# A four-layer transformer block on one core: the layer norms' normalisation on GpSimd, four places for exponentials, and another form of the negated maxima

## The reference

```
x = x + attn0(norm(x))    # one head of 64, causal, biases on q, k, v and out
x = x + ffn0(norm(x))     # x and W rounded to 8-bit e4m3, product in float, plus bias
x = x + attn1(norm(x))    # 16 heads of 16, rotary positions, causal
x = x + ffn1(norm(x))     # token shift: sigmoid(xr Wr) * (relu(xk Wk)^2 Wv)
```

## Time and profile before

| | before |
|---|---|
| median of three runs | 2562.5 us (2561.86 to 2568.54) |
| profiled execution, its own time | 2564.48 us |
| span of its profile | 2562.6 us |
| TensorE busy | 2287.1 us (89%) |
| VectorE busy | 1992.9 us (78%) |
| ScalarE busy | 1512.8 us (59%) |
| GpSimd busy | 528.7 us (21%) |
| mean granted TensorE clock | 0.961 |

### The profile page before, as it was taken

How to read it: one execution, slowest core, us unless ns; L and a number is a source line. 1 busy time by engine, 2 the same in 40 slices (tenths; PEclk the granted TensorE clock), 3 DMA queues, 4 the chain that set the end, 5 groups by cost and what they waited for, 6 DMA issues and landing times.

```text
span 2562.6 us, 51736 instructions
## 1 busy us (share of the span) xinstructions
PE 2287.1 (89%) x19060; PEld 1051.6 (41%) x19060; DVE 1992.9 (78%) x4326; ACT 1512.8 (59%) x2753; POOL 528.7 (21%) x526
## 2 busy tenths in 40 slices
PE   6788878899999999999989999899999989998896
PEld 4444433343444444353434435344344434332344
DVE  4577688888877887879786787887887689889922
ACT  2235437666656657666655565666665567677762
POOL 4444110212114120220304213031211400000011
PEclk7899879999999999999999999999999999999998
DMA  1222211020312222030211302012021121110110
GB/s 47 80 80 71 68 47 43 27 68 17 81 33 50 66 56 60 22 85 12 66 38 37 95 23 80 25 37 70 17 73 33 39 68 45 30 44 23 27 44 27
DMA packets 184102, 125.37 MB, mean 49 GB/s; under 512 B 83120, under 2 KB 183600, under 8 KB 183856
## 3 DMA queue, kind: packets, MB, share of 16 engines
q1 hardware_dynamic: 183088, 121.16, 17.3%
q10 hardware_dynamic: 768, 0.92, 0.1%
HBM read 62.20 MB, written 59.24 MB: 47 GB/s over the span
## 4 chain that ended last, share of the span: by engine, by line
PE 54%; DVE 29%; ACT 6%; issue 5%; DMA 2%; SPq 1%; DVEq 1%; POOL 1%; POOLq 0%; ACTq 0%
DVE mx L1506 20%; PE psum L1815 11%; PE psum L1760 6%; PE psum L1793 5%; PE psum L1726 4%; ACT probs L1266 4%; PE psum L1599 3%; PE psum L1690 2%; PE psum L1846 2%; PE psum L1661 2%; PE psum L1866 2%; PE psum L1835 2%; PE psum L1747 2%; PE psum L1630 2%; DVE xn L1387 2%
## 5 line engine op out<-in xcount | busy, mean ns | idle before, releaser
L1266 ACT ACTIVATE probs<-psum 128x512 f32<-128x512 f32 x2176 | 1142.1, 607 | 506.1 <-PE psum L1793 297.0
L1506 DVE TENSOR_REDUCE mx<-psum 128x1 f32<-128x512 f32 (+2 forms) x2304 | 1285.6, 621 | 143.5 <-PE psum L1760 110.8
L1815 PE MATMUL psum<-probs,vs 128*17 128x512 f32 (+3 forms) x5120 | 592.7, 544 | 3.2 <-ACT probs L1266 2.2
L1760 PE MATMUL psum<-kst,qst 48*128 48x512 f16 (+3 forms) x2560 | 443.5, 356 | 95.7 <-DVE mx L1506 47.3
L1793 PE MATMUL psum<-qst,kst 50*128 50x512 f16 (+3 forms) x2560 | 434.7, 354 | 68.3 <-DVE mx L1506 28.0
L1760 PEld LDWEIGHTS psum<-kst,qst 48*128 48x128 f16 x2560 | 134.0, 94 | 409.4 <-DVE mx L1506 160.8
L1793 PEld LDWEIGHTS psum<-qst,kst 50*128 50x128 f16 x2560 | 130.0, 93 | 384.9 <-ACT probs L1266 150.9
L1815 PEld LDWEIGHTS psum<-probs,vs 128*17 128x17 f32 x5120 | 92.9, 96 | 163.1 <-issue 130.6
L1051 POOL TENSOR_SCALAR vare<-mv 128x4 f32<-128x4 f32 x64 | 15.9, 249 | 682.8 <-DVE mv L1368 682.8
L1767 PE MATMUL psum<-maskq,identh 64*128 64x128 bf16 (+1 forms) x2048 | 133.5, 207 | 0.0
L1080 POOL TENSOR_TENSOR sums<-probs 128x512 f32<-128x512 f32 x12 | 15.3, 1274 | 520.4 <-ACT probs L1220 520.4
(11 more groups left out here) (171 smaller groups left out, 2762.6 us busy)
## 6 DMA issues: line engine op xcount, KB each, us to landing
qk_dram<-parts SPq DMA_DIRECT2D x168, 128.0 KB
qst<-qk_dram SPq DMA_DIRECT2D x128, 96.0 KB, 2.4
kst<-qk_dram SPq DMA_DIRECT2D x128, 96.0 KB, 2.3
v_dram<-vst SPq DMA_DIRECT2D x64, 136.0 KB, 4.6
vs<-v_dram SPq DMA_DIRECT2D x64, 136.0 KB, 2.1
xs<-x_in SPq DMA_DIRECT2D x16, 512.0 KB, 4.1
x_dram<-xs SPq DMA_DIRECT2D x16, 512.0 KB, 2.9
att_dram<-ast SPq DMA_DIRECT2D x64, 128.0 KB, 2.0
```

Of the source, the lines that this page charges most:

```text
L1266: act.activation(dst, src, ACT.Exp, scale=DK1 ** -0.5 / LIFT ** 2).then_inc(S["exp"], 1)
L1506: ins = dve.tensor_reduce(mx1[:, n % 2, 2 * g + odd, tile % TPC, c:c + 1], bank(src, at, at + cols), AX.X, ALU.max)
L1760: ins = pe.matmul(two[odd][:, at:at + cols], qst[rows, qslot, pair, P * (tile % TPC):P * (tile % TPC + 1)], kst[rows, kslot, pair, 0:cols] ...
L1815: ins = pe.matmul(bank(7, off, CH, rows=VW, row=32 * h), vtile[:, h, :], probs[:, HG * (step_no(b, hg, k) % 2) + h, at:at + CH - off], sta ...
```

## The change

- The job `norm` moves from VectorE to GpSimd: the same four `tensor_scalar` instructions with the same waits. Its planned time goes from 1.3 to 2.1 us. The masks that GpSimd makes in the first chunk now come after the first normalisation, and the scaling of late weights on VectorE comes ahead of the statistics instead of the normalisation.
- `probs` gets places for four steps; exponentials wait for the values of step n - 4.
- In `nmax` the odd and even heads are kept apart from the start: two reductions (one for each), one conversion, and one subtraction in place of two. The planned time goes from 0.54 to 0.8 us.
- The layout of the two float16 parts changes with it, so `rows` needs four DMAs of half the size in place of two; planned at 0.3 in place of 0.2 us.
- `out` on VectorE waits for its own job of the block before.

```diff
@@ -42,6 +42,7 @@
 PARTS = 2
 PROWS = len(STORED[0]) * DK1
 LIFT = 4.0
+PSTEPS = 4
 UNIT1 = 32768.0
 REST = 2 * DK1
 MAXROWS = 2
@@ -389,7 +390,7 @@
         add("DVE", "stats", (ln, *c), key(), 1.75, *after, ("norm", same and (ln, *same)), ("root", same and (ln, *same)))
         add("POOL", "root", (ln, *c), key(), 1.33, ("stats", (ln, *c)), ("norm", same and (ln, *same)))
         old = (2, *same) if ln == 0 and same else (ln - 1, *c) if ln else None
-        add("DVE", "norm", (ln, *c), key(), 1.3, ("root", (ln, *c)),
+        add("POOL", "norm", (ln, *c), key(), 2.1, ("root", (ln, *c)),
             ("turn", old))
 
     def turn(ln, *after):
@@ -516,16 +517,16 @@
                 add("DVE", "max d", (*unit, odd), key, 0.07 * reads + 0.533 * size, ("max", unit),
                     ("nmax", block_before(b, hg, q, 2)), free=(("max", unit), odd))
         end = pos - LEAD + UNIT * (q + 1)
-        add("DVE", "nmax", me, end, 0.54, *[("max d", (*unit, odd)) for unit in units for odd in range(2)], ("turnmax", old))
+        add("DVE", "nmax", me, end, 0.8, *[("max d", (*unit, odd)) for unit in units for odd in range(2)], ("turnmax", old))
         add("PE", "turnmax", me, end - 20, 0.07, ("nmax", me), lat=0.1, claim="P", mode="C")
         add("DVE", "turnmax d", me, end - 20, 0.13, ("turnmax", me), ("rows", block_before(b, hg, q, 2)),
             free=("turnmax", me))
-        add("SP", "rows", me, end - 20, 0.2, ("turnmax d", me), lat=2.6)
+        add("SP", "rows", me, end - 20, 0.3, ("turnmax d", me), lat=2.6)
         for k in range(first_step(q), final_step(q) + 1):
             kbs = STEPS[k][1]
             key = pos + UNIT * kbs[0] / TPC
             diagonal = kbs[0] >= TPC * q
-            two = step_before(b, hg, k, 2)
+            two = step_before(b, hg, k, PSTEPS)
             exps = []
             for j, pieces in enumerate(score_jobs(k)):
                 size = sum(cols for *_, cols in pieces) / CH
@@ -584,7 +585,7 @@
     add("DVE", "stats", (3, *c), key(), 1.75, ("add1", (*c, 0)), ("add1", (*c, 1)), ("norm", p and (3, *p)),
         ("root", p and (3, *p)))
     add("POOL", "root", (3, *c), key(), 1.33, ("stats", (3, *c)), ("norm", p and (3, *p)))
-    add("DVE", "norm", (3, *c), key(), 1.3, ("root", (3, *c)), ("turn", p and (3, *p)), ("turn", lent and (2, *lent)))
+    add("POOL", "norm", (3, *c), key(), 2.1, ("root", (3, *c)), ("turn", p and (3, *p)), ("turn", lent and (2, *lent)))
     add("POOL", "carry", c, key(), 0.2, *[("mix", p and (*p, i)) for i in range(2)],
         *[("prod", p and (*p, i)) for i in range(2)])
     turn(3, ("norm", (3, *c)), ("carry", c))
@@ -752,12 +753,12 @@
         kst = sb("kst", [P, KRING, HG // 2, CH], F16)
         qst = sb("qst", [P, QRING, HG // 2, CH], F16)
         vs = sb("vs", [P, 2, NT, HG * VW], F32)
-        probs = sb("probs", [P, 2 * HG, CH], F32)
+        probs = sb("probs", [P, PSTEPS * HG, CH], F32)
         osb = sb("osb", [P, 2, CH], F32)
         ast = sb("ast", [P, 2, TPC, HG * DK1], F32)
         mx1 = sb("mx1", [P, 2, HG, TPC, NQ], F32)
-        nmax1 = sb("nmax1", [P, HG, TPC], F32)
-        nmaxb = sb("nmaxb", [P, 2, MAXROWS, HG // 2, TPC], F16)
+        nmax1 = sb("nmax1", [P, 2, HG // 2, TPC], F32)
+        nmaxb = sb("nmaxb", [P, MAXROWS, 2, HG // 2, TPC], F16)
         nmaxT1 = sb("nmaxT1", [HG * MAXROWS * TPC, 2, P], F16)
         rec = sb("rec", [P, TPC, HG], F32)
 
@@ -831,7 +832,7 @@
 
         def rows_written(wt, b, hg, q):
             n = block_no(b, hg, q)
-            wt.wait_ge(f"rows {n % QRING}", 32 * (n // QRING + 1))
+            wt.wait_ge(f"rows {n % QRING}", 64 * (n // QRING + 1))
 
         def v_loaded(wt, b, hg, c):
             wt.wait_ge(f"load v {hg % 2} {c}", 16 * ((NHG * b + hg) // 2 + 1))
@@ -957,9 +958,10 @@
                     n = block_no(*item)
                     wt.job("turnmax d", item)
                     for odd in range(2):
-                        row = HALF * odd + PROWS
-                        sp.dma_start(qst[row:row + MAXROWS, n % QRING, :, :],
-                                     nmaxT1[16 * odd:16 * (odd + 1), n % 2, :]).then_inc(S[f"rows {n % QRING}"], 16)
+                        for row in range(MAXROWS):
+                            at = 8 * (2 * row + odd)
+                            sp.dma_start(qst[HALF * odd + PROWS + row:HALF * odd + PROWS + row + 1, n % QRING, :, :],
+                                         nmaxT1[at:at + 8, n % 2, :]).then_inc(S[f"rows {n % QRING}"], 16)
                 elif kind == "put att":
                     b, hg, q = item
                     n = block_no(*item)
@@ -1051,11 +1053,29 @@
                     pool.tensor_scalar(vare[:, at, :], mv[:, at, :, 1], EPS, None, ALU.add).then_inc(S["chain p"], 1)
                     wt.wait_ge("chain p", COUNT["root", item])
                     pool.tensor_tensor(rstd[:, at, :], vare[:, at, :], mhalf[:, :], ALU.pow).then_inc(S["root"], 1)
+                    if item != (0, 0, 0) and pieces < KRING:
+                        pool.memset(kst[:, pieces, :, :], UNIT1).then_inc(done, 1)
+                        pieces += 1
+                elif kind == "norm":
+                    ln, b, q = item
+                    old = shared(b, q) if ln < 3 else before(b, q)
+                    at = moments(ln, b, q)
+                    wt.job("root", item)
+                    if ln == 3:
+                        src, dst = xp[:, q % 2, :, :], xn3
+                        wt.job("turn", old and (3, *old))
+                        if (b, q) == (0, 0):
+                            wt.job("turn", (2, 0, NQ - 1))
+                    else:
+                        src, dst = xs[:, q % 2, :, :], xns[lane(b, q)]
+                        earlier = (ln - 1, b, q) if ln else old and (2, *old)
+                        wt.job("turn", earlier)
+                    for t in range(TPC):
+                        ins = pool.tensor_scalar(dst[:, t, :], src[:, t, :], mv[:, at, t, 0:1], rstd[:, at, t:t + 1],
+                                                ALU.subtract, ALU.mult)
+                    ins.then_inc(S["norm"], 1)
                     if item == (0, 0, 0):
                         masks(n)
-                    elif pieces < KRING:
-                        pool.memset(kst[:, pieces, :, :], UNIT1).then_inc(done, 1)
-                        pieces += 1
                 elif kind == "bias0":
                     b, q = item
                     wt.wait_ge("ready", 1)
@@ -1252,10 +1272,10 @@
                                    tiles(home("V1", item), DK1), ACT.Copy).then_inc(S["v1"], 1)
                 elif kind == "exp":
                     b, hg, k, j, odd = item
-                    wt.job("values", step_before(b, hg, k, 2))
+                    wt.job("values", step_before(b, hg, k, PSTEPS))
                     wt.job("scores", item[:4])
                     pieces = score_jobs(k)[j]
-                    at = HG * (step_no(b, hg, k) % 2)
+                    at = HG * (step_no(b, hg, k) % PSTEPS)
                     src = bank(PLAN.home["scores", item[:4]][odd], 0, sum(cols for *_, cols in pieces))
                     if pieces[0][0] == pieces[-1][0]:
                         dst = probs[:, at + 2 * pieces[0][0] + odd, 0:sum(cols for *_, cols in pieces)]
@@ -1349,6 +1369,8 @@
                     old = shared(b, q) if ln < 3 else before(b, q)
                     at = moments(ln, b, q)
                     wt.job("norm", old and (ln, *old))
+                    if item == (3, 0, 0):
+                        later_weights()
                     if ln == 0:
                         x_loaded(wt, b, q)
                     elif ln == 1:
@@ -1367,26 +1389,6 @@
                     for t in range(TPC):
                         ins = dve.bn_aggr(mv[:, at, t, :], stats[:, at, t, :])
                     ins.then_inc(S["stats"], 1)
-                elif kind == "norm":
-                    ln, b, q = item
-                    if item == (3, 0, 0):
-                        later_weights()
-                    old = shared(b, q) if ln < 3 else before(b, q)
-                    at = moments(ln, b, q)
-                    wt.job("root", item)
-                    if ln == 3:
-                        src, dst = xp[:, q % 2, :, :], xn3
-                        wt.job("turn", old and (3, *old))
-                        if (b, q) == (0, 0):
-                            wt.job("turn", (2, 0, NQ - 1))
-                    else:
-                        src, dst = xs[:, q % 2, :, :], xns[lane(b, q)]
-                        earlier = (ln - 1, b, q) if ln else old and (2, *old)
-                        wt.job("turn", earlier)
-                    for t in range(TPC):
-                        ins = dve.tensor_scalar(dst[:, t, :], src[:, t, :], mv[:, at, t, 0:1], rstd[:, at, t:t + 1],
-                                                ALU.subtract, ALU.mult)
-                    ins.then_inc(S["norm"], 1)
                 elif kind == "wf8":
```

(19 more changed lines are left out.)

## The result

| | before | after |
|---|---|---|
| median | 2565.5 us (4 runs) | 2607.8 us (4 runs, 2602.4 to 2614.2) |
| ratio, 95% interval | | 1.0166 [1.0137, 1.0196] |
| profiled execution, its span | 2564.5, 2562.6 us | 2608.1, 2606.0 us |

What follows compares the result with a forecast made beforehand. The prediction took TensorE to bound the kernel, held up in short pieces by a VectorE often one job late. Its terms, -25 + 0 - 5 + 0 - 6 - 3 + 1 = -38, gave 2525 us, range 2492 to 2570.

Steps and rivals of the forecast that it cites:

- part 2: Normalisation joins GpSimd: 0.45 us per instruction, 1.8 us per chunk (ends 1.6 and 2.9), 115 us more on GpSimd; term 0.
- the path of a chunk: Statistics, root, normalise, transposes: 1.38 us become 1.8, cancelled by the hop and turn on VectorE that go; 0.
- Rival A: GpSimd slower than planned: at 0.73 us per instruction TensorE stands before 64 transposes; +13, 2575 us; chance 0.16.
- The planned time: The order's 2.1 us for GpSimd's normalisation should put TensorE's transposes late enough for the assumed 1.8 us.
- Part 1: Normalisation leaves VectorE: 88 us of its time freed, weighted by its 29% of the chain that ended last; -25 us.
- Parts 3 and 5: Negated maxima, planned later at 0.8 us: -5 us; four places for ScalarE's exponentials, ending waits for values: -6 us.
- under 20 us: Sign that the forecast is right: TensorE's wait for the negated maxima, 27.1 us before, falls below this.
- Part 4: Rows by four DMAs: 79 us more of SP's queue, but TensorE never waits for these rows in the steady stretch; 0.
- Start and end: Second chunk normalised five us earlier on GpSimd: -3 us; last normalisations on the chain at 1.8 us: +1 us.

Runs made afterwards that it cites:

- e5: The changed kernel, order untouched, with GpSimd copying the chunk instead of normalising it (normalisation left out of the result): 2508.0 us, ratio 0.9765.
- e4: The changed kernel with the normalisation on GpSimd planned at its measured 4.9 us instead of 2.1, nothing else: 2547.2 us, ratio 0.9918.
- e16: The changed kernel with the normalisation planned at 2.2 us instead of 2.1 and GpSimd copying the chunk instead of normalising it: 2504.7 us, ratio 0.9767.
- e2: The changed kernel with the normalisation back on VectorE, planned at 1.3 us; the other parts of the change stay: 2547.1 us, ratio 0.9918.
- e8: The kernel before with only the other form of the negated maxima, its planned 0.8 us and the rows' four DMAs: 2577.8 us, ratio 1.0046.
- e9: The kernel before with only four places for exponentials and VectorE's wait ahead of an attention output: 2553.5 us, ratio 0.9937.
- e15: The kernel before with VectorE's normalisation planned at 1.2 us instead of 1.3, only the order differing: 2569.1 us, ratio 1.0013.

## Why the prediction was wrong

**The step that failed** is part 2: "I take 0.45 us, near the one-input rows since only one tensor is read". It is 1.22 us, so the term that was put at 0 for the path of a chunk was wrong. The upper bound failed too: it stood at 0.73 us, from the addition of that size, and 1.22 lies beyond both. The nearest rows were of other operations (a cast, a copy, an addition), and none was a `tensor_scalar` over more than 4 columns. Rival A named the mechanism, the point from which it decides (0.65 us) and its sign, but sized it with the same 0.73 us and gave it 0.16. With e5 the assumed price is put to the test: at 0.42 us a pass the same order takes 2508.0 us, better than the forecast. So the price, met by an order that doesn't know it, is worth 100 of the changed kernel's 2608 us, and the sum without this term would have been too cautious, not too bold. Rival A's rule was itself too coarse: with 4.84 us it gives 64 x 2.74 = 175 us, and TensorE waited 92.0 us in 26 places, since many transposes stood late enough anyway.

**The planned time.** The text took 2.1 us as enough for 1.8. With 4.84 us the transposes are planned 2.7 us too early, and TensorE works through its list in order. e4 (2547 us) shows it coming back at the measured price when the order knows it: 61 us in that one pair, 45 by the means; one shift of 0.1 us moved the kernel by 28, so the figure is rough.

**Part 1, the freed VectorE (-25).** The direction holds. TensorE's waits for the maxima in the steady stretch fell from 74.6 to 58.6 us, by a fifth as forecast. e5 and e16 are 39 and 42 us faster than e2, which has the same parts with the normalisation on VectorE. But only 9 us of e5's lead are TensorE's idle time (249.8 against 258.5 us); 28 are its busy time (2254.0 against 2282.2), which part 1 did not speak of, and an order's luck is in both. So the size fits 25 us or more, while the way it took, shorter waits for VectorE alone, isn't shown. At GpSimd's real price nothing of it is left to see: e4 and e2 are equal.

**Parts 3 and 5.** The wait for the negated maxima fell by 6 us (27.1 to 21.0 in the steady stretch; forecast -5), the waits for exponentials from 38.1 to 29.8 (forecast -6), and ScalarE's wait for values from 38.9 us to 0.5. As waits these terms were right. As times of a kernel they drown in the scatter of orders, as e8 and e9 show. The negated maxima stayed just above the "under 20 us" that the text named as a sign. The new form of the maxima isn't shorter, as forecast: two reductions of 168 ns took the place of one of 188, and one subtraction of 175 that of two of 164.

**Part 4.** SP issues the rows' DMAs at 627 ns each, 617 before. TensorE now waits for them four times, 6.5 us, and 9.5 us for the queries loaded behind them, 2.5 before; the term was 0. The four DMAs need not be the cause: e15, with two and another order, has one wait of 7.3 us for the rows, and e2, with four, 3.5 us in six.

**Start and end (-3, +1).** Both had the wrong sign or size. The first transposes start at 13.27 us instead of 10.08, behind the first pass of 4.83 us. The second start at 28.25 instead of 26.68: ahead of their pass GpSimd now works through the first one, the masks and a multiplication of 1.91 us, and the root ends at 22.47 us where the text took 16.88 from the trace of before. At the end three passes of 4.84 us stand on the chain in place of two of 1.39. Counted from the transposes of the fourth last chunk, though, the end is only 1.3 us longer (137.2 against 135.9), with 484 TensorE instructions left instead of 613, so what the passes alone cost there isn't told apart from the new order.

**The range** counted only prices. It left out what a new order does by itself: 14 us in one of two draws with VectorE's normalisation, 28 in one with GpSimd's.

## What to carry to other kernels

Before an operation moves to another engine, take its price from a row of the same operation, over a like number of columns, on that engine; a copy or an addition does not bound it, and where no such row exists the range has to reach to several times the nearest one. Where an order is worked out beforehand, a wrong planned time can cost as much as the operation gains: put in the measured one (here 4.9 for 2.1 us, some 45 to 61 us back). And when a wait goes, look at TensorE's busy time and granted clock too, not at the list of waits alone: over a quarter of e5's gain over the changed kernel stands there. And before a part of such a kernel is judged by a few us, build the same kernel with a planned time shifted by 0.1 us and see how far an order alone moves it.

## What the runs showed of the hardware

GpSimd takes 1.22 us for subtracting one column and multiplying by another over 128x256, 1.08 with constants, 0.94 for one multiplication by a column, and 0.42 for a copy (by the groups above).

VectorE is held up by GpSimd in instructions with two inputs in SBUF as well. The subtraction of the negated maxima takes 175 ns by the median, and once took 2296, at 214.05 us, beside an addition on GpSimd from 213.97 to 216.32; in the kernel before its longest was 169. At the start, a sum of two SBUF inputs that took 0.69 us before took 2.26 beside a multiplication on GpSimd (start, duration):

```profile
L1527 DVE SCALAR_TENSOR_TENSOR nmaxb<-nmax,nmaxb x64: 174/175/2296, 154.2 to 2455.6; 128x16 f16<-128x16 f32 x64
```

```profile
18.79 1.91 POOL L1133 TENSOR_TENSOR xrk<-wqk 128x1024 f32<-128x1024 f32 x1
18.98 2.26 DVE L1357 TENSOR_TENSOR wf<-roped 128x512 bf16<-128x512 f32 x1
```

The VectorE instruction starts behind GpSimd's, and ends at 21.24 us, 0.54 us behind GpSimd's end at 20.70. The kernel before has the same once: a product of two SBUF inputs that started at 13.78 us took 1.26 us, where it takes 0.73 in the changed kernel, and ended 0.55 us behind a GpSimd multiplication that ran from 12.60 to 14.49. The Trainium skill, "SBUF — State Buffer", "Who interferes with whom", says that a VectorE instruction with two SBUF inputs is shut out while a GpSimd instruction reads SBUF; these rows agree.
